# A two-layer transformer on one core: the second chunk's outputs normalised on ScalarE, and the maxima transposed as four column tiles

## What is computed

```
x = x + layernorm(attention0(layernorm(x)))     # 16 heads of 16, causal, low-rank q and kv, rotary
x = x + layernorm(ffn0(layernorm(x)))           # (silu(x Wg * sg) * (x Wu * su)) Wd * sd, 1024 wide
x = x + layernorm(attention1(layernorm(x)))     # 16 heads of 16, causal
x = x + layernorm(ffn1(layernorm(x)))
```

## Time and profile before

| | us |
|---|---|
| median of 3 runs | 1214.76 |
| lowest, highest | 1214.48, 1216.93 |
| the profiled execution | 1218.57 |
| its span in the trace | 1216.8 |

### The profile page before, as it was taken

One profiled execution on the slowest core, in us unless ns is written; L12 is line 12 of the kernel. 1 busy time (PEld: TensorE's weight loads), 2 busy tenths in 40 slices (PEclk: granted clock), 3 DMA queues, 4 the chain that ended last, 5 costly groups with the idle time before them and its releaser, 6 DMA issues.

```text
span 1216.8 us, 36838 instructions
## 1 busy us (share of the span) xinstructions
PE 1135.3 (93%) x14888; PEld 573.3 (47%) x14888; DVE 1025.0 (84%) x2714; ACT 779.6 (64%) x1565; POOL 341.9 (28%) x579
## 2 busy tenths in 40 slices
PE   4768999999999999899998989999999999999996
PEld 3532334445444444655654334444444444465664
DVE  6859999999999784777877999999989888648776
ACT  2452668887888989335452456878888888944332
POOL 5232210121211124343442321113121112434443
PEclk9986999999999999999998999999999999999998
DMA  5263100211200000010220340041120000000001
GB/s 181 78 208 96 60 11 12 68 29 28 55 3 3 3 3 4 1 36 14 66 78 29 107 118 29 7 110 35 29 55 3 3 3 4 4 1 1 18 18 35
DMA packets 31611, 50.03 MB, mean 41 GB/s; under 512 B 7246, under 2 KB 24144, under 8 KB 31432
## 3 DMA queue, kind: packets, MB, share of 16 engines
q1 hardware_dynamic: 25376, 41.95, 12.3%
q0 software_dynamic: 5488, 5.34, 1.6%
q10 hardware_dynamic: 576, 0.39, 0.1%
HBM read 32.56 MB, written 14.68 MB: 39 GB/s over the span
## 4 chain that ended last, share of the span: by engine, by line
PE 68%; DVE 20%; issue 3%; ACT 3%; DMA 2%; POOL 2%; ACTq 0%; POOLq 0%; DVEq 0%
PE ps L1095 66%; DVE m_tile L962 6%; DVE ps L964 3%; PE ps L1269 1%; DVE stats L805 1%; ACT region_p L733 1%; DVE region_p L842 1%; DVE region_p L1016 1%; DVE k_stack L1048 1%; DMA q_stack<-m_rows 1%; PE ps L1090 1%; DVE k_stack L1045 1%; DMA q_parts<-parts 1%; DVE rem L859 1%; DVE region_p L818 1%
## 5 line engine op out<-in xcount | busy, mean ns | idle before, releaser
L733 ACT ACTIVATE region_p<-ps 128x512 f32<-128x512 f32 (+3 forms) x1280 | 591.9, 538 | 158.1 <-PE ps L1095 153.5
L962 DVE TENSOR_REDUCE m_tile<-ps 128x1 f32<-128x512 f32 x768 | 497.6, 684 | 27.4 <-PE ps L1095 24.8
L1095 PE MATMUL ps<-k_stack,q_stack 96*32 96x512 bf16 (+3 forms) x5120 | 400.5, 355 | 14.2 <-DVE m_tile L962 3.8
L1095 PE MATMUL ps<-q_stack,k_stack 99*32 99x512 bf16 (+3 forms) x5120 | 400.1, 349 | 9.2 <-ACT region_p L733 3.8
L1095 PE MATMUL ps<-region_p,v_all 128*17 128x512 f32 (+3 forms) x2560 | 290.2, 529 | 0.5 <-POOL region_p L610 0.5
L964 DVE CUSTOM_DVE_ANT_0 ps<-ps,causal 128x128 f32<-128x128 f32 (+3 forms) x512 | 247.5, 499 | 23.2 <-PE ps L1095 21.5
L1095 PEld LDWEIGHTS ps<-k_stack,q_stack 96*32 96x32 bf16 x5120 | 138.1, 96 | 198.2 <-DVE m_tile L962 61.1
L1095 PEld LDWEIGHTS ps<-q_stack,k_stack 99*32 99x32 bf16 x5120 | 138.1, 96 | 194.1 <-ACT region_p L733 108.5
L610 POOL TENSOR_SCALAR_AFFINE_SELECT region_p<-region_p 128x512 f32<-128x512 f32 x128 | 81.2, 635 | 250.5 <-ACT region_p L733 242.4
L1095 PE MATMUL ps<-region_a,w_ffn 128*128 128x512 f16 x512 | 123.7, 387 | 6.1 <-DVE region_a L850 6.1
L769 ACT ACTIVATE k_stack<-ps,cols 128x512 f32<-128x512 f32 x64 | 44.1, 688 | 109.0 <-PE ps L1095 104.1
(11 more groups left out here) (125 smaller groups left out, 887.1 us busy)
## 6 DMA issues: line engine op xcount, KB each, us to landing
k_parts<-parts SPq DMA_DIRECT2D x16, 384.0 KB, 2.5
q_parts<-parts SPq DMA_DIRECT2D x16, 384.0 KB, 3.2
q_stack<-q_parts SPq DMA_DIRECT2D x32, 192.0 KB
k_stack<-k_parts SPq DMA_DIRECT2D x32, 192.0 KB
q_stack<-q_parts SPq DMA_DIRECT2D x32, 128.0 KB
k_stack<-k_parts SPq DMA_DIRECT2D x32, 128.0 KB
X<-in_x SPq DMA_DIRECT2D x4, 512.0 KB, 6.9
q_stack<-q_parts SPq DMA_DIRECT2D x32, 64.0 KB
```

Of the source, the lines that this page charges most:

```text
L733: nc.scalar.activation(probs[:, o.j % SLOTS, o.h, o.off:CH], psT[:, o.k % TBANKS, o.off:CH], ACT.Exp, scale=SCALE).then_inc(s.exp_done, 1)
L962: nc.vector.tensor_reduce(maximum, scores, AX.X, ALU.max).then_inc(s.ring_free, 1)
L1095: return pe.matmul(o, a, b, start=first, stop=last)
```

## The change

Two things. In each handover, the four normalised tiles of chunk 1 are written by ACT: DVE takes the reciprocal and a product `-mean * rstd` (`output_shift`, one small instruction on 128x4), and ACT writes `rstd * y + shift` with four ACTIVATE Identity of 128x256 that take both factors as per-partition operands. Around it the lists change: on ACT `o_move(6)` stands ahead of the root of chunk 1; on DVE `output_shift(1)` stands ahead of `stats_residual`, `normalize_output(1)` is gone, and `o_stats(3)` stands ahead of `low_parts`. Two waits on `normed` and higher counts on `rstd_done` follow from that. In attention, each of the 32 M pieces becomes four transposes of 32 columns.

```diff
@@ ACT, handover
                 sqrt_branch(k1, 0)
                 o_move(4)
                 o_move(5)
+                o_move(6)
                 sqrt_branch(k1, 1)
-                o_move(6)
+                act.wait_ge(turn[k1].rstd_done, 3)
+                for i in range(TPC, 2 * TPC):
+                    nc.scalar.activation(A[:, i, :], o_tile(i), ACT.Identity, scale=rstd[:, i, 0:1], bias=shift[:, i, 0:1]
+                                         ).then_inc(turn[k1].normed, 1)
                 sqrt_residual(k1, 0)
                 o_move(7)
@@ DVE, handover
+                def output_shift(b):
+
+                    tn = turn[k1]
+                    bs = slice(TPC * b, TPC * (b + 1))
+                    dve.wait_ge(tn.std_done, b + 1)
+                    nc.vector.reciprocal(rstd[:, bs, 0], std[:, bs, 0]).then_inc(tn.rstd_done, 1)
+                    dve.wait_ge(tn.rstd_done, b + 1)
+                    nc.vector.scalar_tensor_tensor(shift[:, bs, 0], mv[:, bs, 0, 0], -1.0, rstd[:, bs, 0], ALU.mult,
+                                                   ALU.mult).then_inc(tn.rstd_done, 1)
+
                 def normalize_output(b):
...
-                    dve.wait_ge(tn.rstd_done, b + 1)
+                    dve.wait_ge(tn.rstd_done, b + 1 + (b > 1))
+                    if b > 0:
+                        dve.wait_ge(tn.normed, TPC * b)
...
                 o_stats(0)
                 normalize_output(0)
                 o_stats(1)
+                output_shift(1)
                 stats_residual(k1, 0)
-                normalize_output(1)
                 normalize_residual(k1, 0)
                 o_stats(2)
                 normalize_output(2)
+                o_stats(3)
                 low_parts(k1, 0)
-                o_stats(3)
                 normalize_output(3)
@@ PE
+            def column_transposes(o, a, identity):
+
+                for j in range(P // 32):
+                    ins = pe.transpose(o[32 * j:32 * j + 32], a[:, 32 * j:32 * j + 32], identity)
+                return ins
...
                     if o.kind == "MT":
                         pe.wait_ge(s.mparts, 4 * (L * NSTEP + o.n + 1))
-                        pe.transpose(ps[:, RING0 + o.ring % RING, 0:P // 2].bitcast(BF16),
-                                     m_parts[:, o.n % 2, :], ident_bf[:]).then_inc(s.ring_filled, 1)
+                        column_transposes(ps[:, RING0 + o.ring % RING, 0:P // 2].bitcast(BF16),
+                                          m_parts[:, o.n % 2, :], ident_bf[:]).then_inc(s.ring_filled, 1)
```

More of the change, by code:

```diff
@@ L224, in build_program @@
         pick = sb("pick", [P, P], BF16)
+        shift = sb("shift", [P, NT, 2], F32)
         ps = ctx.enter_context(nc.psum_tensor("ps", [P, 8, 512], F32))
@@ L421, in o_bank, with o_tile @@
             return 2 + u % 4
+        def o_tile(i):
+            return ps[:, o_bank(i // 2), i % 2 * C:(i % 2 + 1) * C]
         block = ctx.enter_context(nc.Block())
@@ L992, in _ @@
                 k1, k2 = 1 + 2 * L, 2 + 2 * L
-                def o_tile(i):
-                    return ps[:, o_bank(i // 2), i % 2 * C:(i % 2 + 1) * C]
                 def o_stats(b):
```

## The result

| | before | changed |
|---|---|---|
| median of 14 runs each, us | 1216.34 | 1217.77 |
| lowest, highest | 1214.48, 1220.32 | 1216.06, 1220.89 |
| the profiled execution, its span | 1218.57, 1216.8 | 1216.06, 1214.3 |

The account below looks back on a forecast made before the run. PE was taken to bound attention from 176 us and in layer 1, and the end of `low_parts` on DVE the handover. Attention's -4.0 and the handovers' +4.5 gave +0.5 on 1214.76: 1215.3 us, own range 1212.4 to 1218.

Parts of the forecast that it names:

- Price of a transpose: Attention: a whole-array transpose of maxima costs PE 0.21 us more than four tiled ones, 0.10 at entry, 0.105 at exit.
- How much of it reaches the end: Attention of both layers: cheaper transposes on PE's path shorten the kernel by 4.0 us, bounds -5.2 and 0.
- 20 of 24: Attention: of 24 transposes on PE's path, 20 were counted as gaining, 4.2 us.
- Step 2: Handover: DVE's reciprocal waits for the root of chunk 1, so the statistics of `X` start 2.4 us later.
- Step 4: Handover: ACT's four ACTIVATE start 0.47 us apart and delay the residual's root, so DVE loses 0.65 us.
- Step 5: Handover: `normalize_residual` on DVE takes 2.36 us as before and ends 1.2 us late.
- Step 6: Handover: `o_stats(3)` puts 1.6 us ahead of `low_parts`; PE starts the feed-forward 2.8 us later.
- The handover's sum: Both handovers: +2.8 us in layer 1, +1.6 in layer 0, +0.1 for the clock; +4.5, bounds +2.9 and +6.2.
- the rival of the longer cold stretch: Both handovers: longer PE idle brings two stretches at 1.2 GHz, 0.9 to 1.7 us per layer; about 1217.9; chance 0.15.
- DVE takes the whole gain of the maxima: Attention: DVE cannot run faster, leaving only the handover's loss, 1219.4 us; chance 0.13, shared with draining tiles.
- the tiles still drain: Attention: column tiles drain PE as before, leaving only the handover's loss, 1219.4 us; chance 0.13, shared with DVE pacing.
- DVE doesn't wait: Handover: chunk 1's root comes in time, so DVE is not held; 1209.7 us, faster; chance 0.14.

Follow-up runs that it names:

- tiles only: Kernel before, with the 32 transposes of maxima in four column tiles as the only change: 0.9981 of before, -2.3 us.
- handover only: Changed kernel with the transposes of maxima on the whole array again: 1.0043 of before, +5.2 us.
- the last pair of the section on waits: Reordered kernel, DVE's waits removed and `low_parts` ahead of `o_stats(3)`, with M in column tiles and on the whole array: -4.1 and -1.1 us against before.
- root first: Changed kernel with one line moved, the root of chunk 1 on ACT back ahead of `o_move(6)`: 1.0006 of before, +0.7 us.
- no wait: Changed kernel with both roots on ACT back in their earlier places and `stats_residual` ahead of `output_shift(1)` on DVE: 0.9972 of before, -3.4 us.
- no wait and `low_parts` first: Changed kernel with both roots and `stats_residual` back in their earlier order, and `low_parts` ahead of `o_stats(3)`: 0.9966 of before, -4.1 us.
- two tiles of 64: Kernel before, with each transpose of maxima as two tiles of 64 columns: 0.9998 of before, -0.2 us.

## Why the prediction was right, and where it was off

The forecast was 1215.3, or 0.5 us above before; measured are +1.9 [1.0, 2.8] on a median of before that itself came out 1.6 higher with more runs. For both reasons the measured 1217.77 lies near the upper end of the forecast's range, 1218. The kind (no difference of 0.2%), the mechanism and both signs were right. Point by point:

- **Price of a transpose.** 0.21 us expected; 0.32 to 0.22 and 0.16 to 0.06 in the rows. Right. The 0.2 us at the piece that opens layer 1 can't be read off: the granted clock is 0.50 around it, and the four matmuls ahead of it take 3.2 to 3.7 us in the kernels with tiles.
- **How much of it reaches the end.** This is the term that was mis-sized: -4.0 expected. The traces give -2.4 in layer 0, of which the stretch before 176 us has 0.1 and the twelve nearly all of their 2.5. They give -1.4 in layer 1, so -3.9 in all. In layer 1 the steps between two M pieces shrink by about 0.2 in most cases and by nothing in two, and 0.4 is given back ahead of the last piece, where PE now waits 0.4 us for the DMA of the maxima's rows, which before shows no such wait. Also, one of the twelve could gain nothing: the piece at 755.22 comes behind the whole array and ahead of column tiles, and the change only moves the switch from one side to the other. The timed comparisons give less: -2.3 (tiles only), -3.3 (the change against handover only), -3.0 (the last pair of the section on waits). Their mean is -2.9, with an interval of over 1 us on each, so whether 3 or 3.9 is true is open. The step that failed is "20 of 24": I set what layer 1 swallows at a few transposes, and it was over two fifths of that layer's 2.5 us.
- **Step 2, DVE's wait.** 2.1 us expected, 2.02 measured; the root ran behind the move of pair 6, as read off. Right, and root first confirms it.
- **Step 4, the ACTIVATE.** 0.47 apart expected, 0.455 measured (499.05 to 500.87 for four); the second wait 0.65 expected, 0.59 measured. Right.
- **Step 5.** It was to take 2.36 us as before and took 2.04 (501.20 to 503.24). This is most of the reason that PE's idle time is 5.19 and not 5.8, and the delay 2.36 and not 2.8. What is behind it is told in the last section.
- **Step 6.** `low_parts` behind `o_stats(3)` costs 1.6 in the order; swapping it back moved the start by 1.6 in the trace and the time by 2.1.
- **The handover's sum.** +4.5 expected. The profile gives +1.4 and +2.9, so +4.3; timed are +5.2 (handover only) and +4.2 (the change against tiles only). That layer 1's 2.9 meets the expected 2.8 is luck: it is 2.36 of delay and 0.5 of the slow clock, for which I had put 0.1 in both layers together. It was a piece of the rival of the longer cold stretch: the slow stretch did become twice as long in each layer, but its first half fell mostly into idle time.
- **The rivals.** That DVE takes the whole gain of the maxima is refuted by the marks and by tiles only (-2.3 [-3.9, -0.7]); that the tiles still drain, by the rows. That DVE doesn't wait is refuted by the rows; that kernel was built (no wait), and it gains 3.4 where the rival had 5.1.

What stays open is small: the terms of attention and the handovers sum to +0.4, the whole trace from the first M piece on, with the wait near 800 us made equal, to +1.1, and the timed change is +1.9 [1.0, 2.8]. In handover only it is +3.8, +4.8 and +5.2 [3.3, 7.1]. The 0.7 and 0.9 us between the first two sums lie between layer 0's handover and 755 us, and no cause for them was found. A profile shows one execution, and single waits such as that near 800 us differ by 2 us from one to the next.

## What to carry to other kernels

A small instruction with many waiters (here a root of 128x4) belongs ahead of everything on its in-order engine that waits for someone else; when it is moved, look at every wait of that engine's list up to the next such instruction, since curing one can hand the time to the next. Between neighbours in 32-column tiles, a transpose in the same tile size saves the switch in and out, here 0.1 us each way; behind a neighbour on the whole array the same tiles cost the switch instead. So count the places whose neighbours on both sides fit. And before paying to keep TensorE's clock up behind a gap, look whether the slow matmuls are what the next stage waits for: where DVE and POOL pace the start, they are not.

## What the runs showed of the hardware that was not expected

**DVE slows down beside POOL.** The four TENSOR_SCALAR that normalise the residual read and write SBUF and are the same in all kernels. Where POOL only issues DMAs, at the start of the program, they take 1.40 us in before:

```profile
12.04 1.40 DVE L842 TENSOR_SCALAR region_p<-X,mv,rstd 128x256 f32<-128x256 f32 x4
```

In the handover they take 1.90 to 2.63 us. What differs is how long POOL's additions run beside them. In before,

```profile
505.48 2.23 DVE L842 TENSOR_SCALAR region_p<-X,mv,rstd 128x256 f32<-128x256 f32 x4
```

```profile
504.08 2.83 POOL L571 TENSOR_TENSOR X<-X,region_p 128x256 f32<-128x256 f32 x4 [2.40 <-DVE region_p L1016]
```

the overlap is 1.4 us (505.48 to 506.91). One by one these four take 0.85, 0.82, 0.40 and 0.40 us: the two that begin beside POOL's additions need twice the time of the two behind them. In the changed kernel POOL's additions end at 502.52, an overlap of 1.1 us, and the four take 1.90 (0.52, 0.81, 0.41 and 0.40). In the kernel with no wait and `low_parts` first, POOL adds from 499.07 on:

```profile
499.07 2.93 POOL L575 TENSOR_TENSOR X<-X,region_p 128x256 f32<-128x256 f32 x4 [2.63 <-ACT region_p L765]
```

There the overlap is 2.3 us (499.07 to 501.41) and the four take 2.63: 0.41 for the one that is mostly ahead of it, 0.81 to 0.83 for the other three. The longer the overlap, the longer they take. The four with PSUM as source (from 505.51 us in the changed kernel) take 1.90, 0.53 to 0.55 us each as everywhere in these traces, although POOL adds beside them for 1.3 us. The Trainium skill (GPSIMD Engine Reference, Specifications) says that GpSimd shares its SBUF interfaces with VectorE and that they contend for some forms of VectorE's instructions; the durations agree, but no run here changed POOL's work alone, so the cause is argued and not shown.

**The same 24 matmuls** take 5.35 us at the full clock and up to 8.23 behind a long gap (root first, layer 1), depending on where in its idle time PE's clock falls; in before it was 7.03. A gap of the same length was not always followed by a slow stretch: behind 3.03 us of idle time the granted clock fell to 0.50 in both layers of before, and stayed at 1.00 in layer 1 of the kernel with two tiles of 64. **The transfer of the maxima's rows**, 3 KB each, made PE wait between 1.1 and 3.5 us near 800 us; with M on the whole array it was 1.1 to 2.1, in column tiles 1.1 to 3.5, so the form of the M pieces does not explain it.
